# The last eight context projections of a two-layer decoder, placed in later rounds of the first self-attention

## What is computed

```
x = _layernorm(x + _L0_attn_ref(x, ...))            # 16 heads, causal
x = _layernorm(x + _L0_xattn_ref(x, ctx_768, ...))  # 16 heads of 16
x = _layernorm(x + _L0_ffn_ref(x, ...))
x = _layernorm(x + _L1_attn_ref(x, ...))
x = _layernorm(x + _L1_xattn_ref(x, ctx_768, ...))  # 8 heads of 64
x = _layernorm(x + _L1_ffn_ref(x, ...))
```

```
k = (context @ Wk).reshape(b, m, HEADS, DIM_HEAD)
v = (context @ Wv).reshape(b, m, HEADS, DIM_HEAD)
```

## Time and profile before

| | us |
|---|---|
| median of 3 runs | 1243.86 |
| lowest, highest | 1240.53, 1244.32 |
| the profiled execution, its own time | 1234.58 |
| its span | 1232.8 |
| granted TensorE clock, mean of the span | 0.965 |
| PE busy | 1103.5 (90%) |
| DVE busy | 724.9 (59%) |
| ACT busy | 551.0 (45%) |

### The profile page before, as it was taken

How to read it: one execution, slowest core, us unless ns; L and a number is a source line. 1 busy time by engine, 2 the same in 40 slices (tenths; PEclk the granted TensorE clock), 3 DMA queues, 4 the chain that set the end, 5 groups by cost and what they waited for, 6 DMA issues and landing times.

```text
span 1232.8 us, 19658 instructions
## 1 busy us (share of the span) xinstructions
PE 1103.5 (90%) x7370; PEld 700.7 (57%) x7370; DVE 724.9 (59%) x1044; ACT 551.0 (45%) x1044; POOL 111.3 (9%) x133
## 2 busy tenths in 40 slices
PE   5999987888789888699889999999999999898797
PEld 3443343432223322478666778777788787786455
DVE  3431365779899997623255564566757767663213
ACT  2333434155455556712145665456625554561210
POOL 2001023020200000100000000000102001200100
PEclk8999998789899999999999999999999999999799
DMA  5514301200000000000243222133524522200000
GB/s 161 150 69 162 128 9 40 67 28 13 14 14 13 14 1 1 1 18 1 47 113 86 69 69 70 35 77 90 110 52 118 116 69 69 70 2 1 1 18 17
DMA packets 56493, 67.89 MB, mean 55 GB/s; under 512 B 14665, under 2 KB 35922, under 8 KB 56402
## 3 DMA queue, kind: packets, MB, share of 16 engines
q1 hardware_dynamic: 55234, 65.06, 20.1%
q10 hardware_dynamic: 1168, 1.57, 0.4%
HBM read 30.96 MB, written 13.63 MB: 36 GB/s over the span
## 4 chain that ended last, share of the span: by engine, by line
PE 72%; DVE 12%; issue 5%; ACT 4%; SPq 2%; DMA 2%; POOL 1%; ACTq 0%; POOLq 0%; DVEq 0%
PE p_ring L1709 13%; PE p_unit L1709 11%; PE p_out L1856 9%; PE p_ring L1753 8%; PE p_ring L1833 8%; PE p_ring L1730 6%; PE p_out L1822 5%; PE p_ring L1799 5%; DVE halves L1488 4%; DVE prob_a L1502 2%; PE p_ring L1777 2%; PE p_unit L1934 1%; ACT prob_b L1288 1%; PE p_unit L1888 1%; POOL m_z L1234 1%
## 5 line engine op out<-in xcount | busy, mean ns | idle before, releaser
L1302 ACT ACTIVATE prob_a<-p_ring 128x1024 f32<-128x1024 f32 x128 | 130.6, 1023 | 111.8 <-PE p_ring L1799 111.4
L1288 ACT ACTIVATE prob_b<-p_ring,nmax 128x512 f32<-128x512 f32 (+1 forms) x192 | 158.7, 837 | 34.0 <-DVE nmax L1467 33.7
L1467 DVE TENSOR_REDUCE nmax<-p_ring 128x2 f32<-128x1024 f32 (+1 forms) x128 | 156.0, 1220 | 29.4 <-PE p_ring L1753 29.4
L1488 DVE TENSOR_REDUCE halves<-p_ring 128x2 f32<-128x1024 f32 x128 | 155.4, 1218 | 26.5 <-PE p_ring L1777 26.1
L1320 ACT ACTIVATE probT_b<-p_ring 128x512 f32<-128x512 f32 x144 | 84.6, 599 | 192.6 <-PE p_ring L1833 191.0
L1753 PE MATMUL p_ring<-stacks 128*128 128x512 f32 x512 | 151.6, 418 | 9.7 <-ACT prob_b L1288 5.4
L1521 DVE COPY probT_b<-p_ring 128x512 f32<-128x512 f32 x112 | 77.1, 688 | 117.3 <-PE p_ring L1833 117.0
L1833 PE MATMUL p_ring<-ident,prob_b 128*128 128x128 f32 x1024 | 135.3, 275 | 0.9 <-DVE probT_b L1521 0.6
L1833 PEld LDWEIGHTS p_ring<-ident,prob_b 128*128 128x128 f32 x1024 | 116.5, 141 | 24.7 <-issue 16.0
L1799 PE MATMUL p_ring<-x_q,x_kq 32*128 32x512 f32 x512 | 121.6, 658 | 2.3 <-DVE halves L1488 2.1
L1488 DVE TENSOR_REDUCE wide_max<-p_ring 128x2 f32<-128x256 f32 (+3 forms) x64 | 52.6, 823 | 93.6 <-PE p_ring L1771 93.4
(11 more groups left out here) (210 smaller groups left out, 1537.4 us busy)
## 6 DMA issues: line engine op xcount, KB each, us to landing
stacks<-splitH_b SPq DMA_DIRECT2D x80, 128.0 KB, 2.3
stacks<-splitL_b SPq DMA_DIRECT2D x80, 128.0 KB, 2.4
stacks<-x_kd SPq DMA_DIRECT2D x32, 256.0 KB, 4.8
x_kd<-early SPq DMA_DIRECT2D x8, 512.0 KB, 3.1
x_v<-x_vd SPq DMA_DIRECT2D x8, 512.0 KB, 4.1
x_vd<-early SPq DMA_DIRECT2D x6, 512.0 KB, 2.8
a_st<-a_image SPq DMA_DIRECT2D x32, 64.0 KB, 2.8
x_kd<-xT SPq DMA_DIRECT2D x4, 512.0 KB, 3.1
```

The lines of the kernel that those rows point to most:

```text
L1288: ins = nc.scalar.activation(prob_b[:, n % NP_SLOTS, a * 512:a * 512 + w_all], p_scores[:, n % 2, a * 512:a * 512 + w_all], ACT.Exp, bias= ...
L1302: nc.scalar.activation(prob_place(key), slot_of("S2", key), ACT.Exp, accum_out=x0_sums[:, m:m + 1]).then_inc(done["E2"], 1)
L1467: nc.vector.tensor_reduce(nmax[:, n % 4, 0:heads], src, AX.X, ALU.max, negate=True).then_inc(done["M"], 1)
L1488: nc.vector.tensor_reduce(to, src, AX.X, ALU.max, negate=True).then_inc(done["M1"], 1)
```

## The change

The first ten units of the list of `x1_context` (the two `kd` of batch 1, and values and keys of batch 0) keep round 24 as their earliest. The last eight, values and keys of batch 1, get 66, 69, 72 and so on up to 87 as their earliest rounds.

```diff
-        return [unit(*u, at=24, after=[UA("v", "A0", 1, 1), UA("cT", 3, 1)]) for u in order]
+        return [unit(*u, at=24 if n < 10 else 66 + 3 * (n - 10), after=[UA("v", "A0", 1, 1), UA("cT", 3, 1)])
+                for n, u in enumerate(order)]
```

## The result

| | before | change |
|---|---|---|
| median, same chip (6 runs each) | 1239.95 us | 1227.78 us |
| lowest, highest | 1235.63, 1244.32 | 1225.07, 1230.2 |
| ratio to before, 95% interval | | 0.990, 0.987 to 0.993 |
| the profiled execution, its own time | 1234.58 us | 1225.07 us |
| its span | 1232.8 us | 1223.3 us |

The change is faster: 12.2 us by the medians, 9.5 us between the two profiled executions, both of which are faster than their medians. A second measurement (experiment 11) gave 6.7 us, ratio 0.994 (0.991 to 0.996). The two intervals overlap between 0.991 and 0.993, some 9 to 11 us.

What follows compares the result with a forecast made beforehand. PE was taken to bound rounds 38 to 47; SP's issuing, low clock and DVE the weak rounds 68 to 93. Terms: -22.3 + 10.7 = -11.6 us, from 1243.9 to 1232.3 us, range 1225 to 1244.

Steps and rivals of the forecast that it cites:

- Part 1: Rounds 38 to 47, which the eight units leave: 34.3 us become 12.0, a gain of 22.3 us (21.2 to 24.4).
- third rival: Vacated rounds 38 to 47 fall to the low clock: gain 17.9 instead of 22.3, total -7.2, 1236.7 us; chance 0.12.
- Part 2: Rounds 68 to 91, which the eight units enter: +10.7 us in sum, ends +7.7 and +15.1.
- sign of being wrong: The prediction is wrong if rounds 68 to 93 take over 74 us, or the vacated stretch over 17.
- (a): Weak stretch, rounds 68 to 93: units cover PE's two waits for POOL, -5.0 us; TM ends 3 us ahead of the PV.
- (b): Waits of PE for DVE, ahead of `dt` of round 87 and ahead of `mv`: -3.1 us in all.
- (c): Rounds 68 to 91: units take one of three slots, the step three behind waits for ACT's copy: +1.5 us.
- (d): Clock of rounds 68 to 93: -4.5 us for the fall at 209.4 us, -2.5 us for later low spots.
- first rival: Rounds 68 to 93: waits are filled, the low clock stays; total -3.0 us, 1240.9 us; chance 0.17.
- The second: Rival: units land in the low clock in rounds 72 to 91, six costing 4.95 us each; total +8.4, 1252.3 us; chance 0.11.
- Part 3: The rest of the kernel (`mv`, `ma`, `mt` copy, sign loads, POOL order): zero.

Runs made afterwards that it cites:

- experiment 11: The change measured a second time with no new edit, against the kernel before: 1228.86 us, ratio 0.994 (0.991 to 0.996).
- Experiment 1: Kernel before, units unmoved, KL and KF of groups 1 and 2 put behind the POOL clearings that waited for them: 1235.24 us against 1236.62, ratio 0.998.
- experiments 2: The same later KL and KF as in Experiment 1, applied to the change: 1225.4 us, ratio 0.991 to the kernel before.
- experiment 4: The change with its eight units packed into rounds 68 to 79 instead of one in three rounds: 1231.75 us, ratio 0.996 to the kernel before.
- experiment 5: Kernel of Experiment 1 with the matmuls of the sixteen S1 of X0's first group done twice: 1232.78 us, ratio 0.998 to the kernel before.

## Why the prediction was right, and where it was not

**Part 1** said -22.3 us. The vacated rounds gave 23.3 (11.0 us, where I had taken 12.0 and had 9.9 as the lower end; DVE is busy 8.50 of them). The clock stayed at 1.00 in them in this execution, as said, though not in that of experiment 11. But the third rival, which lets them fall, came true just behind them, in rounds 48 to 50, and took 3.1 us back; its price had been put at 4.4. The net is 20.1. I had judged that rival by 160.0 to 167.7 us of before, 7.7 us without large units at 1.00. The vacated stretch is longer, 11.0 us at 1.00 before it falls. The stretch of evidence was shorter than the one it was to speak for, and the earlier trace rows had the warning beside it: 167.7 to 186.4 at 0.92. The Trainium skill's rule ("TensorE: Matmul & The Clock Gate", section "A second HAM failure mode: psum-queue depth-cycling") names the direction that these rounds took; what the runs add is that the fall came 11 us late in one execution and 9 in the other, and that A and B together were 5.3 us longer in the second.

**Part 2** said +10.7 us, with rounds 68 to 93 going from 55.3 to 66. They went to 68.5: +13.2, inside the range given and short of the sign of being wrong (74). The +9.95 of stretch C looks nearer only because C reaches into round 97, and there 3.2 us were gained that the prediction has nowhere. Term by term:

- *(a), (b), (c), the waits:* -6.6 in sum, and the idle time of rounds 68 to 93 fell by 6.4 (12.8 to 6.3). The waits for POOL are gone, the longest for `normed` is 0.8 us after 2.5. The path of (a) held with less margin than worked out. KF of group 2 begins 21.1 us after the first issue of the three KL, where it began 15.5 after it before; that is 5.6 later, and I had said 3.6. TM ends at 195.3 and the PV begins at 196.5 without a wait: a margin of 1.2 us in place of 3. The rows of SP and POOL:

```profile
186.04 2.21 SPq L1081 DMA_DIRECT2D x_kq<-x_qd  x1
...
193.27 1.46 POOL L1194 CAST x_kqF<-x_kq 128x1536 fp32r<-128x1536 f32 x1 [4.44 <-DMA x_kq<-x_qd]
194.68 0.64 POOL L1209 TENSOR_SCALAR_AFFINE_SELECT prob_a<-prob_a 128x512 f32<-128x512 f32 x1
```

  One issue behind an XO took 2.21 us, where one had taken 0.51. I had costed only the waits of SP, not a longer issue.
- *(c)* in its place: the longest wait left in C, 1.3 us, is for `raw`, whose copy stands on ACT behind that of the unit of round 84. A unit's copy can delay others on ACT; my sum priced the ring alone. With the two waits of units at the ring (0.5 and 0.3) it makes 2.1 us, where 1.5 was said.
- *(d), the clock:* -7.0 was said for rounds 68 to 93. There the other work got 6.4 us shorter (42.5 of busy time, and 62.1 less the units' 26.0) and one unit 1.7 longer: -4.7. **The direction was right, the size too large and the reason wrong.** I had the fall at 209 us follow from the idle of 5.0 us; it had in fact come at 207.3, while PE waited. Experiment 1 takes the wait away, and the clock falls two rounds later and is 0.73 over C. Where all eight units stood in C, its clock was 0.86 to 0.96, and the low piece at the hand-over shrank from 13.6 us to 3.4 (the change) and to none (experiments 2 and 4). So the better clock comes with the units themselves, and belongs to them and not to (a). How they bring it isn't shown. Rounds 48 to 50 of the change, the hand-over of experiment 1 and the wait behind the last unit of experiment 4 all come after a stretch with small matmuls only (S1, S2, PV and transposes) and a clock of 1.00: 11.00, 13.8 and 8.2 us long, PE busy for 9.93, 11.97 and 6.96. But before, in B, small matmuls with two `wo` among them went on at 1.00 for longer:

```profile
160.10:183.25 23.15, 19.23 (x163) 10.93 (x164) 17.52 (x32) 10.57 (x14) 5.79 (x12) 1.00 0.05 12
```

- Hence the split of the gain by cause is also other than written: filling POOL's wait is worth 2.5 us by itself in the profile of experiment 1 and 1.4 between its medians, not 5.0 and 4.5 more for the clock behind it.

**The first rival**, waits filled and clock not, would have given 1240.9 us; the clock of 0.91 rules it out. **The second**, units in the low clock, came for one unit of eight (4.69 us). **Part 3**, nothing elsewhere, held behind C (974.5 and 974.6 us), but not between round 93 and its end: these rounds took 9.4 us at 0.65 before and 6.1 at 1.00 in the change. Part 3 looked at waits alone, and the clock there is a term that it left out.

So the total of -11.6 us came near the 9.5 between the profiles with some luck: A gave 2.2 us less than said and rounds 68 to 93 cost 2.5 more, and 3.2 came from rounds that the sum had at nothing (0.6 more lie ahead of A and behind C). The measured gain, 12.2 and 6.7 us between medians, lies on both sides of the forecast. The absolute number, 1232.3 us against 1227.8 measured, is off by 4.5 us, of which 3.9 are the kernel before: its median was 1243.9 over the three runs shown and 1239.95 over six.

**Open.** What exactly brings the clock down. It fell inside a wait of 3.5 us (before), and also where no wait in the 11 us ahead was over 0.5 us and PE was busy for 9.93 of them (the change), so a long wait isn't needed. Whether the form of the matmuls, their spacing or the short waits decide was not told apart; experiment 5 was meant for it and its dose was too small. That the same kernel ran B at 0.96 in one execution and at 0.84 in another says that something outside the kernel's order has a part in it.

## What to carry to other kernels

Work that has no fixed place, and is dense, is worth more in a stretch where PE idles or runs at a low clock than where PE is the bound: here the same unit cost 3.0 us in rounds 38 to 47, about 2 in 52 to 61, and 1.2 in 68 to 91. The first dose takes the cover (10.0 of 24.3 us paid), a second pays nearly in full (20.3 of 24.3), so move as much as fills the waits. Spreading it over the weak stretch did better than packing it, and leaving one unit behind better than moving all, each by a few us that the intervals don't fully part. Price the place that is vacated too: its clock can fall once the dense work is gone. Before you blame a low clock on the wait ahead of it, remove the wait alone and look. And read a second execution of the same kernel before you split a gain of 10 us into terms of 2.

## What the hardware showed that I had not expected

- The clock fell at no wait: after 11.0 us with PE busy for 9.93, at 1.00, it went to 0.53 for 7.21 us. The Trainium skill ("TensorE: Matmul & The Clock Gate", section "HAM oscillation — how this bites in real kernels") describes falls by a long wait for data between bursts of matmuls; this one doesn't agree with that, since the longest wait ahead of it was 0.5 us.
- The granted clock of one stretch with the same instructions differs from execution to execution (0.96 and 0.84 in B of the change, 38.9 and 43.7 us), while the whole kernel's median moves by 1.1 us between the two measurements of the change.
- Two more 32x512 matmuls in an S1 cost 0.23 us after 0.50 for the first two (experiment 5).
- A DMA issue on SP, 0.51 us for most of KL's, took 2.21 us as the second behind the second XO, and 2.13 us at the same place in experiment 11.
